# One product of a gated recurrence moved from GpSimd to VectorE, in a two-layer sequence kernel

## The reference

```python
pre = einsum('btd,df->btf', layernorm(x), W) + b
i_pre, f_pre, o_pre, z = split(pre, 4)
i_gate = 10 * tanh((i_pre + input_bias) / 10);  f_gate = -softplus(f_pre)
o = sigmoid(o_pre);  tz = tanh(z)
# for each token:
m_next = maximum(f_t + m, i_t)
c = exp(f_t + m - m_next) * c + exp(i_t - m_next) * tz_t
n = exp(f_t + m - m_next) * n + exp(i_t - m_next)
h = o_t * (c / (n + 1e-6))
# after the scan:
x = x + h / sqrt(mean(h ** 2) + 1e-8) * scale
```

## Time and profile before

| | |
|---|---|
| Median of 3 runs | 368.25 us (367.87 to 512.96) |
| The profiled execution's own time | 366.78 us |
| Its span in the trace | 365.0 us |
| TensorE busy in the span | 314.6 us, 86% |
| VectorE, ScalarE, GpSimd busy | 72%, 63%, 59% |
| Share of the chain that ended last | PE 47%, POOL 20%, DVE 15%, ACT 8%, issue 7% |
| L786 in all | 8 instructions, 25.8 us, mean 3.227 us |
| L582 in all | 8 instructions, 23.4 us, mean 2.930 us |

### The profile page before, as it was taken

One profiled execution on the slowest core, in us unless ns is written; L12 is line 12 of the kernel. 1 busy time (PEld: TensorE's weight loads), 2 busy tenths in 40 slices (PEclk: granted clock), 3 DMA queues, 4 the chain that ended last, 5 costly groups with the idle time before them and its releaser, 6 DMA issues.

```text
span 365.0 us, 4805 instructions
## 1 busy us (share of the span) xinstructions
PE 314.6 (86%) x1760; PEld 270.8 (74%) x1760; DVE 261.2 (72%) x433; ACT 228.2 (63%) x365; POOL 216.4 (59%) x166
## 2 busy tenths in 40 slices
PE   0799399495957999999999999999999975799996
PEld 0677268364747978897889788978898865689896
DVE  2879998928795689658974898398839884592331
ACT  1579556658736588766878587948684733481640
POOL 1285763689459835974497629762986299238000
PEclk9999869679896999999999999999999999799999
DMA  7980000000000010000100010000000000000001
GB/s 200 393 299 3 0 1 0 0 2 0 0 0 3 30 67 21 0 31 29 59 0 31 29 58 2 27 5 29 0 16 14 32 0 29 31 0 31 29 1 59
DMA packets 10936, 14.22 MB, mean 39 GB/s; under 512 B 672, under 2 KB 10144, under 8 KB 10656
## 3 DMA queue, kind: packets, MB, share of 16 engines
q1 hardware_dynamic: 10480, 13.63, 10.6%
q10 hardware_dynamic: 432, 0.27, 0.5%
HBM read 9.71 MB, written 4.19 MB: 38 GB/s over the span
## 4 chain that ended last, share of the span: by engine, by line
PE 47%; POOL 20%; DVE 15%; ACT 8%; issue 7%; DMA 2%; SPq 0%; DVEq 0%; POOLq 0%
PE mm_ps L192 10%; PE mm_ps L191 10%; PE mm_ps L190 10%; POOL rec L786 5%; POOL g L804 3%; PE z_ps L190 3%; PE z_ps L192 3%; PE z_ps L191 3%; POOL rows L819 2%; DVE rec L546 2%; PE t_ps L297 2%; POOL rows L825 2%; ACT xn L386 2%; DMA rows<-x 2%; DVE rec L582 2%
## 5 line engine op out<-in xcount | busy, mean ns | idle before, releaser
L190 PE MATMUL z_ps<-w_hi,y_hi 128*128 128x256 f32 x256 | 74.6, 291 | 0.4 <-DVE y_lo L631 0.4
L192 PE MATMUL z_ps<-w_hi,y_lo 128*128 128x256 f32 x256 | 73.1, 285 | 0.0
L191 PE MATMUL z_ps<-w_lo,y_hi 128*128 128x256 f32 x256 | 72.8, 284 | 0.0
L414 ACT ACTIVATE y<-mm_ps,b_all 128x512 f32<-128x512 f32 x64 | 44.0, 687 | 20.2 <-PE mm_ps L246 9.1
L631 DVE TENSOR_TENSOR y_lo<-y,y_hi 128x512 fp32r<-128x512 f32 x64 | 42.6, 683 | 19.2 <-ACT y_hi L417 19.1
L190 PEld LDWEIGHTS z_ps<-w_hi,y_hi 128*128 128x128 f32 x256 | 49.1, 192 | 1.3 <-DVE y_lo L631 1.2
L191 PEld LDWEIGHTS z_ps<-w_lo,y_hi 128*128 128x128 f32 x256 | 49.5, 193 | 0.1
L192 PEld LDWEIGHTS z_ps<-w_hi,y_lo 128*128 128x128 f32 x256 | 49.0, 191 | 0.0
L190 PE MATMUL mm_ps<-gt_hi,w_hi 128*128 128x512 f32 x112 | 45.5, 406 | 1.4 <-ACT y L414 1.4
L192 PE MATMUL mm_ps<-gt_hi,w_lo 128*128 128x512 f32 x112 | 45.3, 404 | 0.0
L191 PE MATMUL mm_ps<-gt_lo,w_hi 128*128 128x512 f32 x112 | 45.2, 404 | 0.0
(11 more groups left out here) (109 smaller groups left out, 700.1 us busy)
## 6 DMA issues: line engine op xcount, KB each, us to landing
out<-rows SPq DMA_DIRECT2D x16, 256.0 KB, 2.1
rows<-x SPq DMA_DIRECT2D x7, 512.0 KB, 9.8
q<-fc_q SPq DMA_DIRECT2D x2, 1024.0 KB, 12.5
wg_raw<-w_gates SPq DMA_DIRECT2D x2, 512.0 KB, 8.3
s<-fc_scales SPq DMA_DIRECT2D x1, 1024.0 KB, 12.2
wg_raw<-fc_scales SPq DMA_DIRECT2D x1, 1024.0 KB, 10.8
rows<-x SPq DMA_DIRECT2D x2, 256.0 KB, 4.4
scale_bc<-scale_row ACTq DMA_DIRECT2D x1, 128.0 KB, 5.7
```

Of the source, the lines that this page charges most:

```text
L190: pe.matmul(dst, wh[w_at], ah[a_at], start=start, stop=False)
L191: pe.matmul(dst, wh[w_at], al[a_at], start=False, stop=False)
L192: return pe.matmul(dst, wl[w_at], ah[a_at], start=False, stop=stop)
L414: act.activation(y[:, j % YBUFS], mm_ps[:, j % 4], ACT.Silu, bias=b1_all[:, j:j + 1]).then_inc(silu_done, 1)
```

## The change

GpSimd's `oc_over` and its semaphore `ocr_ready` go. VectorE's `h` becomes two instructions behind `newton`: `refined`, r' = (2 - d r) r, written to plane 1, and then h = r' (o c), a `tensor_tensor` of planes 1 and 2 into plane 0, which waits for `oc_ready`, the end of `o_times_c`. All three are 128 x 1024 float32 with both inputs in SBUF. The order of everything else is as it was.

```diff
@@ VectorE
+            def refined(c):
+                v = rec[c % 2][:, 1]
+                dve.wait_ge(newton_done, at(c, 2, 1))
+                dve.scalar_tensor_tensor(out=v, in0=rec[c % 2][:, 0], scalar=2.0, in1=v, op0=ALU.subtract,
+                                         op1=ALU.mult, reverse0=True).then_inc(newton_done, 1)
+
             def h(c):
-                d = rec[c % 2][:, 0]
-                dve.wait_ge(newton_done, at(c, 1, 1))
-                dve.wait_ge(ocr_ready, at(c, 1, 1))
-                dve.scalar_tensor_tensor(out=d, in0=d, scalar=2.0, in1=rec[c % 2][:, 2], op0=ALU.subtract,
-                                         op1=ALU.mult, reverse0=True).then_inc(h_done, 1)
+                refined(c)
+                dve.wait_ge(newton_done, at(c, 2, 2))
+                dve.wait_ge(oc_ready, at(c, 1, 1))
+                dve.tensor_tensor(rec[c % 2][:, 0], rec[c % 2][:, 1], rec[c % 2][:, 2], ALU.mult).then_inc(h_done, 1)
@@ GpSimd
-            def oc_over(c):
-
-                oc = rec[c % 2][:, 2]
-                pool.wait_ge(oc_ready, at(c, 1, 1))
-                pool.wait_ge(recip_done, at(c, 2, 2))
-                pool.tensor_tensor(oc, oc, rec[c % 2][:, 1], ALU.mult).then_inc(ocr_ready, 1)
-
@@
             o_times_c(0)
-            oc_over(0)
             input_times_z(1)
...
             o_times_c(1)
-            oc_over(1)
             input_times_z(2)
             base(0)
...
                 o_times_c(t - 1)
-                oc_over(t - 1)
                 if exists(t):
                     input_times_z(t)
                 base_bias(t - 2)
```

More of the change, by code:

```diff
@@ L141, in layer @@
         denom_ready, recip_done = sem("denom_ready"), sem("recip_done")
-        oc_ready, ocr_ready = sem("oc_ready"), sem("ocr_ready")
+        oc_ready = sem("oc_ready")
         newton_done, h_done, ht_ready = sem("newton_done"), sem("h_done"), sem("ht_ready")
```

## The result

The changed kernel takes 375.38 us (median of 4 runs, 373.35 to 376.65) against 368.06 us; the ratio is 1.0212, 95% interval 1.0185 to 1.0238. The ratio is to 367.60 us, the median of the kernel before with its profiled execution and without one of 512.96 us. It is slower by some 2%. The forecast was 373.3 us in a range of 366.5 to 377.5, with 0.79 for within 2% and 0.16 for slower by more. The profiled execution's own time was 374.6 us and its span 372.8, against 366.78 and 365.0.

What follows compares the result with a forecast made beforehand. TensorE's own work was taken as the bound: busy 86% of the span, 36.91 of 38 us in the steady loop. Prologue +3.4, steady loop +3.65 and end -2.0 gave +5.05 us, so 373.3 us, range 366.5 to 377.5.

Steps and rivals of the forecast that it cites:

- Prologue, to `g_turned(1)`: Chunks 0 and 1: the bias delays L576, h(1) is 2.8 us late, plus 0.6 for low clock; +3.4 us, bounds +1.25 and +4.8.
- t = 3: First steady loop step: h comes 0.95 us later, less at most 0.2 us of slack before TensorE's transposes; +0.8 us.
- t = 4, 5, 6, the late h: Steady loop steps where TensorE already waits 0.9 us for `x_low`: h 0.95 us later each, 2.85 us in all.
- falls of the clock in the loop: Steady loop: the forecast sum had none, taking the clock as granted in full throughout the loop.
- End: the late h at t = 7: At t = 7 the late h reaches TensorE but is not passed on, as TensorE idles before `g_turned(6)` anyway.
- End: GpSimd and VectorE free of the bias behind h(6): At the end, VectorE's scans free of L825 let GpSimd's work come earlier; 0.6 us gained, between 0 and 0.95.
- End: the product less in chunk 7: At t = 8 h ends at 311.4 instead of 312.80; 1.4 us less, all passed on to TensorE.
- Who gets the turn: VectorE and GpSimd instructions with two SBUF inputs alternate; in the steady loop h ends 0.95 us later, +3.65 us in all.
- rival 1: VectorE keeps the turn from `refined` to h and L825 waits for both; sum -3.5, 364.8 us; chance 0.14.
- rival 3: Prologue absorbs its part: L825 misses L576 of chunk 1, which keeps to 1.4 us; +2.9, 371.2 us; chance 0.12.
- rival 2: Clock falls in the loop after TensorE's 1.85 us wait, 1.7 us a step, five times; +13.5, 381.8 us; chance 0.07.
- the forecast case: Whole kernel: turns alternate, h comes late in prologue and loop, earlier at the end; +5.05 us, 373.3 us; chance 0.62.

## Why the prediction was right, and where it was short

The sum by its own terms, against the profile after:

| Term | Forecast | Measured |
|---|---|---|
| Prologue, to `g_turned(1)` | +3.4 | +2.9 |
| t = 3 | +0.8 | +1.0 |
| t = 4, 5, 6, the late h | 3 x 0.95 | 3 x 1.0 |
| falls of the clock in the loop | none | +3.0 (2 x 1.5) |
| End: the late h at t = 7 | 0 | +0.98 |
| End: GpSimd and VectorE free of the bias behind h(6) | -0.6 | -2.7 |
| End: the product less in chunk 7 | -1.4 | -1.4 |
| End: behind the transposes at t = 8 | 0 | +0.98 |
| Sum | +5.05 | +7.8 |

The two shares of -4.11 us at t = 8 are those of the kernels with a part of the change. In the whole kernel they are -3.67 before `o_times_c` and -0.43 behind its start.

- **Who gets the turn** was right. The alternation read from three instructions in the prologue gave h's end to 0.03 us, and the kernel with the bias moved confirms it against rival 1. One sign was off: `input_times_z` did not start behind the reciprocal and stand for 3.3 us, it started a microsecond later behind exp(i), took 2.50, and ended where the forecast had it, 3.49 us after L576's start.
- **The prologue** was right in size (+2.9 and +2.5 in the two profiles, forecast +3.4), and its place differs between executions. I had the bias issued 0.5 us ahead of L576, and L576 behind it at 2.9 us. In the first profile both were issued in the same instant (84.52 and 84.53), L576 took 1.21 us, the sign that I had given for rival 3, and `y_low` behind it stood there instead. In the second the bias was first and L576 took 2.22. Since VectorE's instructions before h follow one another in one queue, the loss is there in both.
- **The end** was right in sum, by luck. Its term for what GpSimd and VectorE gain ahead of h(7) was 0.6 us with a bound of 0.95, and it measured 2.7. I had reasoned only from the scans, and GpSimd's own instructions ran clear of VectorE as well (the root of L812 took 1.97 us before and 1.00 after, the four of `base` 3.13 and 2.17). This was taken back by two delays that I had put at nothing: the late h at t = 7 was passed on, 0.98 us, and 0.98 more was lost behind t = 8, where the low clock lasted longer (to 324.6 us, 4.9 us after the transposes start, before 2.8).
- **The clock** is the step that failed. The forecast put its falls in the loop at nothing, and the granted clock below 1.00 in the loop was my own sign of being wrong: it came, and cost 3.0 us. I gave rival 2 a chance of 0.07 on one case: a wait of 2.20 us at whose middle the clock was 1.00. That row was true and proved little, because it is a matter of chance. In the profiles of the changed kernel (two) and of the new form in chunks 2 to 6, 10 waits of 1.85 to 1.91 us have 7 falls; two of 1.36 and 1.43 us have none, and the 0.9 us waits of the kernel before have none. The 2.2 us wait near the end fell in four kernels out of eight. The price of one fall, 1.5 us, was near the 1.7 that I gave; the number was two or three, not five. Why the same wait is followed by a fall in one step and not in another stays open here.
- **The bounds** were added up wrongly. The ends of the terms as stated give 1.25 + 3.4 - 2.4 = +2.25 and 4.8 + 4.3 - 1.3 = +7.8, that is 370.5 to 376.1 us, not 371.5 to 375.1. The measured 375.38 lies outside the stated ends and inside the right ones, but by a cause that none of the terms held.

So the forecast case and rival 2 came together, and the sum missed 2.8 us. That the measured time lies in the range is in part luck: the range reached past the terms' ends for chunk 1's sake, not for the clock's, and the clock's cost had room in it because only two or three falls came. A rival that is a threshold in my sum ("decides only if 1.85 us is too long") and that my own change doubles towards deserves more than 0.07.

## What to carry to other kernels

Moving an instruction between VectorE and GpSimd moves more than its time: with two SBUF inputs on either side, each one in the stretch costs a turn of the other engine, so count the alternating turns on the way to the result that is waited for, and then order the other engine's idle work behind that result. Here one semaphore wait for h was worth 3.6%, in the old form 1.8%, and the moved product without it was a loss. The product is worth moving only chunk by chunk: the fastest version keeps it on GpSimd in the prologue. And when TensorE already waits a microsecond in each step, a second one may cost two and a half, because the clock may fall behind it.

## What the runs showed of the hardware that I had not expected

- Behind equal waits of 1.9 us in one program the granted clock fell in some steps and not in others, and in another execution of the same program in other steps. A fall in the loop lasted about 3.4 us and cost 1.5.
- Seven matmuls without a use in each such wait (1.79 us of work in the profile) kept the clock up and made the kernel faster, 375.8 to 371.4 us.
- GpSimd instructions with one input pay beside VectorE, and VectorE hardly: the four of `base` took 6.17 us beside VectorE and 2.71 mostly clear of it, while VectorE's products beside them took 1.41 instead of 1.21.
